# A two-layer macaron kernel on one core: five plain gathers at the end, W_in's column sums inside the last routed slot, and some down products ahead of the first mixing

## What is computed

```python
x = x + 0.5 * _L0_ffn_ref(_layernorm(x), gate_w, shared_gate, ..., r_down)
x = x + _L0_attn_ref(_layernorm(x), W_in, b_in, conv_w, ..., W_out, b_out)
x = x + 0.5 * _L0_ffn_ref(_layernorm(x), gate_w, shared_gate, ..., r_down)

# _L0_ffn_ref: a shared expert for all tokens, and one of 8 routed experts for each
shared_out = _swiglu(x, shared_gate, shared_up, shared_down)   # silu(x@wg.T) * (x@wu.T) @ wd.T
top_id = argmax(x @ gate_w.T);  score = sigmoid(max(x @ gate_w.T))
routed_out = sum over e of _swiglu(where(top_id == e, x * score, 0), r_gate[e], r_up[e], r_down[e])

# _L0_attn_ref: x @ W_in + b_in, causal convolution of 4 taps, a linear recurrence of 16 states
# (a fixed kernel over time), silu, @ W_out + b_out
```

## Time and profile before

| | us |
|---|---|
| median of 3 runs | 868.56 (866.89 to 869.25) |
| the profiled execution, its own time | 869.6 |
| its span in the trace | 867.8 |
| PE busy in the span | 827.1 (95%) |
| DVE busy | 484.1 (56%) |
| POOL busy | 466.7 (54%) |
| ACT busy | 390.6 (45%) |

### The profile page before, as it was taken

How to read it: one execution, slowest core, us unless ns; L and a number is a source line. 1 busy time by engine, 2 the same in 40 slices (tenths; PEclk the granted TensorE clock), 3 DMA queues, 4 the chain that set the end, 5 groups by cost and what they waited for, 6 DMA issues and landing times.

```text
span 867.8 us, 16211 instructions
## 1 busy us (share of the span) xinstructions
PE 827.1 (95%) x5302; PEld 719.2 (83%) x5303; DVE 484.1 (56%) x979; ACT 390.6 (45%) x766; POOL 466.7 (54%) x444
## 2 busy tenths in 40 slices
PE   4999999999999999999999999999999999999993
PEld 3778988888888878888888888888788888888883
DVE  7788853333333336768998986777333333333452
ACT  4643334343343434557687776233343343434330
POOL 6528870333334068849999982786332233230785
PEclk9999999999999999999999999999999999999998
DMA  9963553555554246210010015255354555521665
GB/s 307 326 254 104 176 170 122 195 191 206 180 212 151 81 93 115 37 25 13 21 43 25 25 51 194 73 170 171 128 169 159 193 200 199 188 66 37 130 140 149
DMA packets 53158, 119.07 MB, mean 137 GB/s; under 512 B 6443, under 2 KB 41397, under 8 KB 48757
## 3 DMA queue, kind: packets, MB, share of 16 engines
q0 software_dynamic: 17776, 75.25, 27.8%
q1 hardware_dynamic: 34834, 43.15, 15.2%
q10 hardware_dynamic: 498, 0.02, 0.0%
HBM read 83.25 MB, written 35.14 MB: 136 GB/s over the span
## 4 chain that ended last, share of the span: by engine, by line
PE 73%; POOL 13%; DVE 5%; issue 4%; DMA 3%; ACT 0%; POOLq 0%; DVEq 0%; SPq 0%; ACTq 0%
PE bank L424 21%; PE bank L426 21%; PE bank L425 21%; POOL acc L1929 4%; PE bank L629 4%; DVE v L1541 2%; PE bank L598 2%; DMA wr_hi<-w_routed 2%; POOL xs_sorted L1855 2%; PE bank L491 2%; POOL wr_lo L1899 2%; POOL yr L2046 1%; POOL v L1827 1%; PE bank L502 1%; POOL hT_lo L1831 1%
## 5 line engine op out<-in xcount | busy, mean ns | idle before, releaser
L1899 POOL TENSOR_TENSOR wr_lo<-wr_raw,wr_hi 128x3072 fp32r<-128x3072 f32 x14 | 95.4, 6816 | 96.9 <-DMA wr_hi<-w_routed 88.6
L424 PE MATMUL bank<-wr_hi,xT_hi 128*128 x312 | 130.2, 417 | 1.0 <-POOL wr_lo L1899 1.0
L1929 POOL DMA_INDIRECT acc<-ys_sorted,pos x52 | 86.2, 1658 | 81.0 <-issue 51.4
L1206 DVE TENSOR_TENSOR hT_lo<-bank,hT_hi 128x512 fp32r<-128x512 f32 x78 | 53.9, 691 | 124.7 <-ACT hT_hi L881 124.7
L426 PE MATMUL bank<-wr_lo,xT_hi 128*128 x312 | 123.4, 396 | 0.0
L1499 DVE TENSOR_TENSOR hf<-sg,bank 128x512 f32<-128x512 f32 x78 | 53.6, 687 | 124.4 <-PE bank L426 124.4
L425 PE MATMUL bank<-wr_hi,xT_lo 128*128 x312 | 122.9, 394 | 0.0
L424 PE MATMUL bank<-xT_hi,ws_hi 128*128 128x512 f32 x256 | 102.6, 401 | 2.2 <-DVE xT_lo L1206 2.2
L425 PE MATMUL bank<-xT_hi,ws_lo 128*128 128x512 f32 x256 | 100.9, 394 | 0.0
L426 PE MATMUL bank<-xT_lo,ws_hi 128*128 128x512 f32 x256 | 100.7, 393 | 0.0
L908 ACT ACTIVATE sg<-bank 128x512 f32<-128x512 f32 x64 | 38.2, 597 | 130.5 <-PE bank L426 112.8
(11 more groups left out here) (248 smaller groups left out, 2163.2 us busy)
## 6 DMA issues: line engine op xcount, KB each, us to landing
wr_raw<-w_routed POOLq DMA_DIRECT2D x16, 1536.0 KB, 7.2
wr_hi<-w_routed POOLq DMA_DIRECT2D x16, 1536.0 KB
rows<-xs_sorted SPq DMA_DIRECT2D x78, 128.0 KB, 2.3
ys_sorted<-rows SPq DMA_DIRECT2D x78, 128.0 KB
xg<-xT_kept SPq DMA_DIRECT2D x12, 512.0 KB
xT_kept<-xTf SPq DMA_DIRECT2D x9, 512.0 KB, 2.6
acc<-x SPq DMA_DIRECT2D x8, 512.0 KB, 9.9
xs_sorted<-zeros POOLq DMA_DIRECT2D x4, 1024.0 KB, 8.4
```

Source lines behind the costliest of these rows:

```text
L424: pe.matmul(o, a_hi, b_hi, start=start, stop=False, skip_group_check=True)
L1206: return dve.tensor_tensor(o, full, f32(h), ALU.subtract)
L1899: pool.tensor_tensor(wr_lo[:, e % 2, :], wr_raw[:, :], f32(wr_hi[:, e % 2, :]), ALU.subtract).then_inc(s_wl, 1)
L1929: pool.indirect_dma_start(out=acc[:, tt, :], out_offset=None, in_=ys_dram, in_offset=bass.IndirectOffsetOnAxis(ap=pos[:, tt:tt + 1], axis= ...
```

## The change

The change has four parts.

- Five groups are plain now: `PLAIN` is 3, 0, 4, 1, 5. The order of the gathers is 6, 3, 7, 0, 4, 2, 1, 5, `yr` grows from 12 to 20 tiles, and DVE adds group 0 and group 1 as well. The fourth plain group writes `yr` where `wr_hi` was, so POOL waits ahead of it until the last slot's result is copied (`s_ye`). SP stores in the new order, and the two halves of group 5 are the last stores.
- `w_in_sums` runs in layer one's last slot, between the transposes of `hf` and the down products.
- In layer one's last group, the down products of blocks 0 and 1 for tiles 0 and 1 (12 instructions) come ahead of the first mixing, and those of blocks 2 and 3 for tiles 2 and 3 alone (12) stand behind `w_in_part`.
- `SCALED`: three of the scalings move to earlier blocks, in both layers.

The diff, cut to its core:

```diff
-        yr = sb("yr", [P, (NT // GT - NH - 1) * GT, H], F32, final)
+        yr = sb("yr", [P, 5 * GT, H], F32, final)
...
-        ADDED = [{}, {3: (LATE[0],)}, {2: (LATE[1],), FB: (LATE[2],)}]
-
-        GATHERED = (6, 7, LATE[0], 0, LATE[1], 1, LATE[2], 2)
-
-        def added(g): return 1 + LATE.index(g)
+        PLAIN = (LATE[0], 0, LATE[1], 1, LATE[2])
+        GATHERED = (6, LATE[0], 7, 0, LATE[1], 2, 1, LATE[2])
+        ADDED = [{}, {3: PLAIN[0:1]}, {0: PLAIN[1:2], 2: PLAIN[2:3], FB: PLAIN[3:5]}]
+
+        def added(g): return 1 + PLAIN.index(g)
...
-                    if first and half == 1 and L == 0:
-                        w_in_sums()
...
                     if L == 0 and half == 1 and last:
                         pe.wait_ge(s_ainit, 1)
+                        shared_down(L, g, 0, range(2))
+                        shared_down(L, g, 1, range(2))
                         pe.wait_ge(s_h, 4 * NG)
                         mix_chunk(0, 0, 0)
                         mix_chunk(0, 1, 0)
...
-                        for a in range(2):
-                            for fb in range(FB):
-                                shared_down(L, g, fb, range(2 * a, 2 * a + 2))
-                            if a == 0:
-                                pe.wait_ge(s_wiol, 2)
-                                w_in_part(0, 0)
-                                w_in_part(0, 1)
+                        shared_down(L, g, 2, range(2))
+                        shared_down(L, g, 3, range(2))
+                        shared_down(L, g, 0, range(2, 4))
+                        shared_down(L, g, 1, range(2, 4))
+                        pe.wait_ge(s_wiol, 2)
+                        w_in_part(0, 0)
+                        w_in_part(0, 1)
+                        shared_down(L, g, 2, range(2, 4))
+                        shared_down(L, g, 3, range(2, 4))
...
                 m_transpose_h(L, NS - 1)
+                if L == 0:
+                    w_in_sums()
                 m_down(L, NS - 1, now)
...
                 pe.wait_ge(s_wio, 48)
-                pe.wait_ge(s_ye, NS)
...
-            SCALED = ({}, {1: (4,), FB: (5,)}, {1: (6,), 3: (7,)}, {})
+            SCALED = ({}, {1: (4,), 3: (5,)}, {0: (6,), 2: (7,)}, {})
...
             for g in GATHERED:
-                if g not in LATE:
+                if g not in PLAIN:
                     gather(g, s_ga[g])
                     continue
+                i = PLAIN.index(g)
+                if i == 3:
+                    pool.wait_ge(s_ye, 2 * NS)
...
-            for g in GATHERED[:6]:
-                if g in LATE:
+            for g in GATHERED:
+                if g == LATE[-1]:
+                    continue
+                if g in PLAIN:
...
-            g = GATHERED[-1]
-            sp.wait_ge(s_ga[g], 2 * 16 * GT)
-            sp.dma_start(tiles(ot, g), tiles(acc, g)).then_inc(s_out, 16)
```

More of the change, by code:

```diff
@@ L1445, in add_rows @@
                     dve.wait_ge(s_add, 2 * (c_s(1, g) + 1))
-                dve.tensor_tensor(tiles(acc, g), tiles(acc, g), yr[:, bass.ds(LATE.index(g) * GT, GT), :],
+                dve.tensor_tensor(tiles(acc, g), tiles(acc, g), yr[:, bass.ds(PLAIN.index(g) * GT, GT), :],
                                   ALU.add).then_inc(s_fad, 1)
@@ L2041, in _ @@
             for g in GATHERED:
-                if g not in LATE:
+                if g not in PLAIN:
                     gather(g, s_ga[g])
                     continue
+                i = PLAIN.index(g)
+                if i == 3:
+                    pool.wait_ge(s_ye, 2 * NS)
                 for t in range(GT):
                     pool.indirect_dma_start(
-                        out=yr[:, LATE.index(g) * GT + t, :], out_offset=None, in_=ys_dram,
+                        out=yr[:, i * GT + t, :], out_offset=None, in_=ys_dram,
                         in_offset=bass.IndirectOffsetOnAxis(ap=pos[:, g * GT + t:g * GT + t + 1], axis=0)
```

## The result

The changed kernel takes 861.93 us (median of 6 runs, 861.67 to 862.49). The kernel before took 867.3 in the runs made beside it (six with the first three, 866.29 to 869.25). The ratio is 0.9932, 95% interval 0.9923 to 0.9942: 0.68% faster, 5.9 us of 868. The forecast was a gain of 5.0 us. The profiled execution took 862.49, its span is 860.6 (before: 867.8).

The account below looks back on a forecast made before the run. PE bounds most of the kernel; POOL's issuing, one landing and one store set the end. Terms 1.50 + 0.93 + 2.56 = 4.99 us off 869.6 give 864.6, or 863.5 us against the median 868.56; range 861.6 to 866.4.

Parts of the forecast that it names:

- the tail's sum: End of the program, from the gathers on: 2.56 us earlier, bounds 0.8 to 4.6 us.
- W_in's sums: Layer one's last slot: the moved sums cover PE's 1.50 us wait for `hT_lo`; gain 1.50 us, bounds 0 to 1.50.
- The down products: First mixing: twelve products moved ahead cover PE's 0.93 us of idle time; gain 0.93 us, bounds 0 to 0.93.
- The first rival: Attention behind the mixing: DVE's and POOL's work swallows the gain, 0.93 becomes -0.4; time 864.8; chance 17%.
- POOL's issuing: Layer two's gathers: three adding and five plain groups take 50.35 us instead of 54.69, 4.34 us less.
- two more adds then cost 0 to 1.8 us. I take 0: Layer two's gathers: DVE's two extra adds may hold POOL up, up to 0.9 us each; taken as 0.
- a sign of being wrong: Layer two's gathers: plain groups in a row taking over 6 us would show the prediction wrong; 5.0 to 6.0 expected.
- The tail's end: End of the program: set by routed slots done, POOL's 54.69 us of issuing, then one landing and one store.
- of the 4.34 us, 1.8 go back into DVE's add and the sum of the halves: Behind the last gather's landing: added DVE work takes back 1.8 of POOL's 4.34 us, leaving 2.56.
- The scalings: Both layers: three scalings at earlier blocks; up to 1.0 us won or 1.37 us delay, taken as 0.
- The rivals on the tail: End of the program: DMA engines bind, tail gains nothing, 866.1 us, 13%; or late landing makes it slower, 871.4, 5%.
- the slower rival: Group 5's last rows: DMA backlog makes them land 9.9 us late, 871.4 us; decides from 7.0 us on; chance 5%.

Follow-up runs that it names:

- the part alone: Kernel before with only the twelve down products put ahead of the first mixing; ratio 0.9984 (0.9975 to 0.9993), -1.4 us.
- the round trips: Kernel before with one or two small stores to HBM, each waited for, on SP ahead of the last store; ratios 1.0004 and 1.0002.
- the two that changed it: Kernel before with two small waited-for stores ahead of the last store, ratio 1.0002; changed kernel with POOL waiting for its last gather's landing, ratio 0.9960.
- group 1 held: Changed kernel with DVE's addition of group 1 held back until group 5's second tile landed; 861.48 us, ratio 0.9920 to the kernel before.

## Why the prediction was right or wrong

The direction and the course up to the gathers were right; the tail's sum was too small, and its mechanism wrong.

- *W_in's sums.* Forecast 1.50. By the trace 1.8, by the runs 1.6 (0.8 to 2.3). The mechanism was right, and the runs don't tell 1.5 from 1.8. In the trace the size was short, as the gap holds more than its idle time: the later start of the down products was 1.21 us, not 1.36, and 1.8 + 1.2 = 3.0 us went at the sums' old place, restart included, not 2.86.
- *The down products.* Forecast 0.93; by the trace 1.2, by the runs 1.4 (0.6 to 2.2). Right in mechanism, and the free 1.09 us of the gap were read as 0.93. The first rival (the attention swallows it, and the time rises by 0.4) is refuted by the part alone.
- *POOL's issuing.* Forecast 50.35 us, measured 51.18. The term at fault is "two more adds then cost 0 to 1.8 us. I take 0": two of the five additions did hold a tile up, 1.0 us each, where in before two had cost 0.92 (the tile at 853.12) and 0.38 (the one at 845.31, 1.33 us long). The reason for the 0 was that group 5's addition would now come behind the last gather and group 1's take its place. That came true; but group 4's, which had cost the 0.38, now fell onto a tile's start and cost 0.99. How the rest of the 0.83 us splits up stays open: DVE's smaller operations hold tiles up as well (1.9 us in all in after), and a part of that was in the lengths taken from before. With all this two of the plain groups in a row took 6.36 and 6.24 us (839.81 to 846.17, and to 852.11 + 0.30), over the 6 that the prediction had named as a sign of being wrong. Where an addition falls against the tiles is decided by tenths: in the kernel with the sums alone, the same addition as in before began 0.02 us ahead of a tile instead of 0.19 and held nothing up. POOL issued for 53.8 us there, for 54.7 in before. Held tiles end 0.81 to 0.87 us behind the addition's end, nearly their whole own length of 0.95. So the cost is the addition's end less the tile's start, less some 0.1 us: at most 1.04 in these traces, and nothing for a tile already begun. The Trainium skill (SBUF — State Buffer, the section on its two separate sides) gives the pair of ports for a whole instruction to whichever engine starts first, and a DVE operation with two inputs in SBUF takes part only against a GpSimd operation that reads SBUF. The rows agree where the addition starts first. Where the tile does, they don't: an addition that begins inside a tile still takes 1.22 to 1.23 us (849.73 beside the tile of 849.35).
- *The tail's end.* The step that failed is "the store of the group gathered last goes out at 861.44 ... and the span ends at 867.8. So the end is set by ... then one landing and one store", and with it "of the 4.34 us, 1.8 go back into DVE's add and the sum of the halves". The last store ended nothing: SP waited another 3.2 us for the engines' leaving. The end is POOL's last issue and 8.5 us. Landing, addition, halves and stores lie beneath that; nothing was given back. What POOL saves counts in full: 54.69 - 51.18 = 3.5 us against a forecast of 2.56, and 3.3 (2.2 to 4.4) in the runs, an interval that holds both figures; that it is the 3.5 rests on the fixed 8.5 and the round trips. Two errors met here, 0.83 too much in POOL's issuing and 1.8 too little behind it.
- *The scalings.* Forecast 0, measured +0.5 (-0.3 to +1.3): nothing that the runs can tell.
- *The rivals on the tail.* The last rows landed 2.35 us behind their issue, so no backlog. A landing costs nothing up to 2.35 + 0.9 = 3.25 us (0.9 is the room), so the slower rival would have decided not from 7.0 us on but from about 3.25 + 5.8 = 9.0.

The gains by the runs, 1.6 + 1.4 + 3.3 - 0.5 = 5.8, are 0.8 us above the forecast's 5.0. The profiled pair's own times differ by 7.1 us; 1.04 of it is that before's execution was above the median, as the prediction had subtracted. That the total came out within 1 us is luck in part: the 1.8 us given back for nothing and the 0.83 too much saved on POOL offset each other.

What stays open: why POOL's DRAIN at the end needs 8.3 us. The one at the start of the program, behind four small memsets and no transfer, takes 0.17 us, so it isn't the instruction's fixed price; whether it is the indirect transfers that cost it, no run here shows, as none had a POOL that ended without any.

## What to carry to other kernels

Before saying what ends a program, look past the last store: if SP still waits for the other engines behind its last landing, find the engine whose last instruction lies at a fixed distance from the end in several kernels, and shorten that one's list. Work of the others that ends within that distance is free, so shift it there. And take the start of a late stage from several traces: one pair was 0.9 us off here. An idle time in PE's rows is short by what the modelled length of the product ahead of it overlaps its successor: take start to start, less the usual spacing.

## What the runs showed of the hardware

- POOL's leaving takes 8.5 us from the end of its last instruction to the end of the span, the same in all kernels but the two that changed it, and it starts only once its last wait is over (11.0 us with a wait of 2.4 us for a landing). It is a DRAIN of 8.28 us; at the start of the program the same instruction takes 0.17.
- A DVE addition of 128x1024 (1.22 us) with both operands in SBUF keeps POOL from starting an indirect transfer's issue: up to 1.99 us for a tile instead of 0.95. Subtractions of 128x512 (0.68 us) do it, too (up to 1.38 us for a tile). An operation with one operand in a bank doesn't (at most 1.00), and a tile begun before the addition stays at 0.95 (849.35, group 1 held).
- A semaphore increment in POOL's queue behind its last indirect transfers was seen by DVE before those transfers were issued (addition at 848.41, the last two issues at 848.80 and 850.76).
- Five plain groups of four tiles in a row were issued in 5.0 to 6.1 us a group, held-up tiles included. The last rows landed 3.0 us behind their issue with a store of 512 KB issued 0.8 us ahead of that, and 1.8 us behind it with the store 1.9 us behind that.
